# Second layer's local attention: token tiles on the array's row groups instead of heads, keys computed once

## The reference, cut to what matters

```python
def local_gqa_attn(x, wq, wk, wv, wo):
    q = split_heads(x @ wq, H)             # H = 16, HD = 8
    k = split_heads(x @ wk, KVH)           # KVH = 4
    v = split_heads(x @ wv, KVH)
    q, k = (rope(q, BASE_L), rope(k, BASE_L))
    q, k = (qk_norm(q), qk_norm(k))        # x * rsqrt(mean(x * x) + EPS)
    k, v = (repeat_kv(k), repeat_kv(v))
    i = jnp.arange(x.shape[1])
    diff = i[:, None] - i[None, :]
    mask = (diff >= 0) & (diff < WIN)      # WIN = 32
    return merge_heads(sdpa(q, k, v, mask)) @ wo
...
x = x + global_latent_attn(rmsnorm(x, norm1_w), ...)
x = x + local_gqa_attn(rmsnorm(x, norm2_w), ...)
```

## Time and profile before

| | |
|---|---|
| median of 3 runs | 993.89 us (993.09 to 997.41) |
| the profiled execution, its own time | 992.87 us |
| its span (first to last instruction) | 990.7 us, so 2.2 us lie around it |
| TensorE's granted clock in it | 0.996 of 2.4 GHz |
| PE, DVE, ACT, POOL busy | 938.4, 533.3, 539.8, 149.3 us |
| second layer's local attention | heads about 361 to 389, loop 389 to 436, end to about 448 us |

### The profile page before, as it was taken

One profiled execution on the slowest core, in us unless ns is written; L12 is line 12 of the kernel. 1 busy time (PEld: TensorE's weight loads), 2 busy tenths in 40 slices (PEclk: granted clock), 3 DMA queues, 4 the chain that ended last, 5 costly groups with the idle time before them and its releaser, 6 DMA issues.

```text
span 990.7 us, 23062 instructions
## 1 busy us (share of the span) xinstructions
PE 938.4 (95%) x10112; PEld 424.0 (43%) x10112; DVE 533.3 (54%) x870; ACT 539.8 (54%) x767; POOL 149.3 (15%) x164
## 2 busy tenths in 40 slices
PE   7799999999999989889999999989999999999998
PEld 4467643433333335654443444434333333443443
DVE  4566646533324366775665455556666666424554
ACT  6044546889999846646666612275555454545121
POOL 3101120501001003130110400001232232005000
PEclk9999999999999999999999999999999999999999
DMA  7644050100000000000000076000000000002651
GB/s 209 210 123 137 21 225 0 44 2 2 2 2 2 2 1 1 4 3 1 0 1 0 18 169 129 29 1 1 2 2 2 2 2 2 0 1 64 153 118 53
DMA packets 16764, 43.18 MB, mean 44 GB/s; under 512 B 4844, under 2 KB 5292, under 8 KB 15244
## 3 DMA queue, kind: packets, MB, share of 16 engines
q1 hardware_dynamic: 15692, 39.51, 15.0%
q10 hardware_dynamic: 972, 2.20, 0.7%
HBM read 36.91 MB, written 4.55 MB: 42 GB/s over the span
## 4 chain that ended last, share of the span: by engine, by line
PE 79%; ACT 9%; DVE 6%; issue 2%; DMA 2%; SPq 1%; ACTq 0%; POOL 0%; DVEq 0%; POOLq 0%
PE ps L1639 78%; ACT nrr L816 1%; ACT nrr L818 1%; DMA stf<-aux 1%; ACT nsq L809 1%; DVE work L1363 1%; DVE mxq L1258 1%; ACT work L986 1%; ACT work L897 1%; ACT nrr L826 1%; ACT nrr L823 0%; DMA stf<-scr_k 0%; DVE aux L1413 0%; DMA x<-in_x 0%; PE ps L2087 0%
## 5 line engine op out<-in xcount | busy, mean ns | idle before, releaser
L1639 PE MATMUL ps<-rq,stf 32*64 32x512 f32 (+4 forms) x4096 | 197.6, 438 | 6.4 <-DVE stf L1316 2.6
L1639 PE MATMUL ps<-work,vbuf 64*32 64x128 f32 (+6 forms) x2992 | 186.7, 400 | 2.0 <-ACT work L897 1.2
L1639 PE MATMUL ps<-hz,wsb 128*128 128x512 f32 (+1 forms) x352 | 158.4, 599 | 7.0 <-ACT work L1058 4.4
L957 ACT ACTIVATE work<-ps 128x1024 f32<-128x1024 f32 x144 | 139.4, 1023 | 13.2 <-PE ps L1639 8.6
L1639 PEld LDWEIGHTS ps<-rq,stf 32*64 32x64 f32 x4096 | 88.8, 131 | 112.0 <-issue 79.3
L1019 ACT ACTIVATE work<-ps 128x1024 f32<-128x1024 f32 x72 | 73.7, 1025 | 75.6 <-PE ps L1639 75.6
L1639 PEld LDWEIGHTS ps<-work,vbuf 64*32 64x32 f32 (+1 forms) x2992 | 60.0, 107 | 111.1 <-issue 59.1
L1639 PEld LDWEIGHTS ps<-hz,wsb 128*128 128x128 f32 (+1 forms) x352 | 61.6, 186 | 83.4 <-issue 67.9
L1639 PE MATMUL ps<-bsb 128*64 128x512 bf16 (+1 forms) x378 | 82.1, 386 | 11.7 <-DVE mxq L1258 3.8
L1065 ACT ACTIVATE work<-ps 128x512 f32<-128x512 f32 x48 | 28.7, 597 | 117.1 <-PE ps L1639 117.1
L1341 DVE TENSOR_TENSOR work<-work,csb 128x1024 f32<-128x1024 f32 (+1 forms) x40 | 40.7, 1018 | 96.0 <-ACT work L957 95.6
(11 more groups left out here) (200 smaller groups left out, 1167.4 us busy)
## 6 DMA issues: line engine op xcount, KB each, us to landing
stf<-scr_w SPq DMA_DIRECT2D x32, 256.0 KB, 4.7
stf<-scr_w SPq DMA_DIRECT2D x64, 128.0 KB, 3.4
stf<-scr_q SPq DMA_DIRECT2D x12, 192.0 KB
wsb<-in_w SPq DMA_DIRECT2D x1, 2192.0 KB, 12.8
rq<-in_rq SPq DMA_DIRECT2D x2, 1024.0 KB, 10.1
stf<-scr_k SPq DMA_DIRECT2D x9, 204.0 KB
rq<-scr_k SPq DMA_DIRECT2D x6, 204.0 KB
hz<-scr_k SPq DMA_DIRECT2D x6, 204.0 KB
```

The source lines that it names most:

```text
L957: nc.scalar.activation(probs_of(n)[:, 2 * k:2 * k + 2].rearrange("p h s -> p (h s)"), two(slot(2 * n + k)), ACT.Exp, scale=SCALE).then_inc ...
L1639: return nc.tensor.matmul(o, l, r, start=start, stop=stop, skip_group_check=True)
```

## The change

Queries and keys of the local attention are laid out anew: row group j of the 128 partitions holds token tile 4c + j of each chunk c instead of head hd. So the keys, which four heads share, are computed once: two units of KW = 160 columns a tile (32 of the tile before and its own 128), `k_l`, and four query units, one for each head, `q_l`. A score product streams the queries of all four heads. A step's scores are 12 products in place of 32: 64 keys over 4 x 96 queries, 64 keys over 4 x 64, and the 32 keys of the tile before over 4 x 32. All are issued behind both exponentials of the step before. The sums over values change their last part from 64 to 32 rows. The group keys are four masks of 640 columns in place of nine. The rotary table of the second attention is laid out by tile. Nothing else of the program changes. In the diff, UNITS_L is 6 and unit_width is 320 for m < 2 and 512 after; the first `local_heads` shown is DVE's, the second PE's (ACT and POOL have one each of their own).

```diff
-        LOCAL_COUNTS = dict(GLOBAL_COUNTS, sc=32, ex=32, mk=16, pv=16, oe=4, oc=4, o=6)
+        LOCAL_COUNTS = dict(GLOBAL_COUNTS, mm=6, t=6, rot=6, sq=6, var=6, ln=6, r=6, kn=2, kz=4,
+                            sc=32, ex=32, mk=16, pv=16, oe=4, oc=4, o=6)
...
-            rope_load(1)
+            sp.dma_start(rope_l, rope_k.rearrange("k p c s -> p k c s")).then_inc(s_rope, 16)
...
+            def local_heads():
...
+                for m in range(UNITS_L):
+                    rt_, w, o = rope_t[:, m % 4], unit_width(m), pair(AL, m)
...
+                    for i in range(2):
...
+                        ins = nc.vector.tensor_tensor(to, src, turn, ALU.mult)
+                    ins.then_inc(q["t"], 1)
...
+                    if m >= 4:
+                        local_group_keys(m - 4)
...
-                    if n % 2 == 0 and n // 2 + 1 < len(PASSES):
-                        group_keys(AL, *PASSES[n // 2 + 1])
+                    if n < 2:
+                        local_group_keys(2 + n)
...
+            def local_heads():
...
+                def keys(m):
+                    for i in range(2):
+                        for j in range(4):
+                            for k in range(CB):
+                                at = (CB * m + k) * CH + j * P - WIN_L
+                                skip = max(0, -at)
+                                ins = mm(bank(pair(AL, m) + i)[32 * j:32 * j + 32, k * KW + skip:(k + 1) * KW],
+                                         wk[i][:, 0:32], z[:, at + skip:at + KW])
+                    ins.then_inc(q["mm"], 1)
+
+                def queries(m):
+                    hd = m - 2
+                    for i in range(2):
+                        for j in range(4):
+                            ins = mm(bank(pair(AL, m) + i)[32 * j:32 * j + 32].rearrange("p (c s) -> p c s", c=NC),
+                                     wq[i][:, 32 * hd:32 * hd + 32], by_row_group[:, j])
+                    ins.then_inc(q["mm"], 1)
+
+                for m in range(UNITS_L + 1):
+                    if m < UNITS_L:
+                        pe.wait_ge(n_z, normed(n, 2 * m + 1 if m < 2 else NC - 1))
+                        if m >= 3:
+                            pe.wait_ge(q["ln"], was["ln"] + m - 2)
+                        (keys if m < 2 else queries)(m)
+                    if 2 <= m < 2 + NC:
...
+                        values_by_token(v, bank(6 + v % 2), w_("l_wv")).then_inc(q["v"], 1)
+                    if m == UNITS_L:
+                        stay_awake(pair(AL, m - 2) + 1, 5)
+                    if m:
+                        pe.wait_ge(q["sq"], was["sq"] + m)
+                        mm(bank(pair(AL, m - 1))[:, 0:unit_width(m - 1)], c_("head"),
+                           rope_t[:, (m - 1) % 4, 1, 0:unit_width(m - 1)]).then_inc(q["var"], 1)
...
                 def scores(n):
...
+                    if n == 0:
+                        pe.wait_ge(q["q"], was["q"] + G)
...
+                    def block(j, lo, m, q0, w):
+                        rows = slice(32 * j, 32 * j + 32)
+                        o = bank(j)[lo:lo + m, 0:G * W_L].rearrange("p (h s) -> p h s", h=G)
+                        at = HB if m == WIN_L else 0
+                        first = 0 if m == WIN_L else WIN_L + lo
+                        return mm(o[:, :, at:at + w], kz_l[rows, g, c, first:first + m],
+                                  q_l[rows, :, c * P + q0:c * P + q0 + w])
+
+                    if n == 1 or n == 2:
+                        stay_awake(4, 6)
+                    if n:
+                        pe.wait_ge(q["ex"], was["ex"] + 2 * n)
+                    for j in range(4):
+                        block(j, 0, HB, 0, W_L)
+                        block(j, HB, HB, HB, HB)
+                    for j in range(4):
+                        if (n % 2, j) != (0, 0):
+                            ins = block(j, P - WIN_L, WIN_L, 0, WIN_L)
+                        if j % 2:
+                            ins.then_inc(q["sc"], 1)
...
                 def values(n):
...
+                    for j in range(4):
+                        block(j, 0, HB, 4 * st + j, 0, 0, W_L, opens)
+                        ins = block(j, HB, HB, 4 * st + j, HB, 0, HB, opens)
+                    for j in range(4):
+                        if st + j:
+                            ins = block(j, P - WIN_L, WIN_L, 4 * st + j - 1, 0, HB, WIN_L, False)
```

More of the change, by code:

```diff
@@ L49 @@
 W_A, W_L = P + WIN_A, HB + WIN_L
+KW = P + WIN_L
+UNITS_L = 2 + G
 NEG = -1e30
@@ L933, in normed_heads @@
                         ins.then_inc(q["vf"], 1)
-                    if a == AG and 3 <= m < 3 + NC:
+                    if 3 <= m < 3 + NC:
                         hidden_factor(2, m - 3)
+            def local_heads():
+                was = WAS[AL]
+                for m in range(UNITS_L + 1):
+                    if m < UNITS_L:
+                        rt_, w = rope_t[:, m % 4], unit_width(m)
+                        act.wait_ge(q["rot"], was["rot"] + m + 1)
+                        nc.scalar.activation(rt_[:, 1, 0:w], rt_[:, 0, 0:w], ACT.Square).then_inc(q["sq"], 1)
+                    if m:
+                        rt_, w = rope_t[:, (m - 1) % 4], unit_width(m - 1)
+                        act.wait_ge(q["var"], was["var"] + m)
+                        if m > 4:
+                            act.wait_ge(q["kn"], was["kn"] + m - 4)
+                        nc.scalar.activation(rt_[:, 2, 0:w], bank(pair(AL, m - 1))[:, 0:w], ACT.Ln, bias=eps[:, 1:2])\
+                            .then_inc(q["ln"], 1)
+                        act.wait_ge(q["ln"], was["ln"] + m)
+                        nc.scalar.activation(rt_[:, 2, 0:w], rt_[:, 2, 0:w], ACT.Exp, scale=-0.5).then_inc(q["r"], 1)
+                    if 2 <= m < 2 + NC:
+                        c = m - 2
+                        act.wait_ge(q["v"], was["v"] + c + 1)
+                        act.wait_ge(s_vz, 6)
+                        for g in range(NG):
+                            ins = nc.scalar.activation(
+                                vq[:, 4 * c:4 * c + 4, g // 2, g % 2, columns_of(g, False)],
+                                bank(6 + c % 2)[:, 0:4 * KVH * D].rearrange("p (t g d) -> p t g d", t=4, g=NG)
+                                [:, :, g], ACT.Copy)
+                        ins.then_inc(q["vf"], 1)
             def rotated_consumed(a, n):
@@ L1079, in _ @@
             norm(4)
-            normed_heads(AL)
+            local_heads()
             local_soft()
@@ L1812, in normed_heads @@
                             pe.wait_ge(n_z, normed(n, c))
-                        if a == AG and m < 3:
+                        if m < 3:
                             if m == 0:
@@ L1827, in normed_heads @@
                         if v < 2:
-                            pe.wait_ge(n_z, first(n - 1, 2 + v) if a == AG else 4 * n + 3 + v)
+                            pe.wait_ge(n_z, first(n - 1, 2 + v))
                         else:
@@ L1958, in values @@
                     if n == 0:
-                        pe.wait_ge(q["ln"], was["ln"] + 2 * NC)
                         pe.wait_ge(q["vf"], was["vf"] + NC)
@@ L1964, in values, with block @@
                     opens = g % 2 == 0
[L1965 to L1979 removed]
+                    def block(j, lo, m, t, q0, at, w, start):
+                        rows = slice(lo, lo + m)
+                        cells = heads[rows, j, 0:G * W_L].rearrange("p (h s) -> p h s", h=G)
+                        own = qd[rows, T:T + WIN_L] if t < 0 else vq[rows, KT * b + t, g // 2, g % 2]
+                        return mm(by_tile((6 if lo else 4) + st, j)[:, :, q0:q0 + w], own, cells[:, :, at:at + w],
+                                  start, False)
+                    for j in range(4):
+                        block(j, 0, HB, 4 * st + j, 0, 0, W_L, opens)
[3 more added lines that the diff above has]
+                            ins = block(j, P - WIN_L, WIN_L, 4 * st + j - 1, 0, HB, WIN_L, False)
+                        elif opens:
+                            ins = block(j, P - WIN_L, WIN_L, -1, 0, 0, WIN_L, False)
                     ins.then_inc(q["pv"], 1)
@@ L2288, in rope_tables, with turns @@
 def rope_tables():
-    q = np.zeros((2, 2, P, S), np.float32)
-    for n, base in enumerate((1000000.0, 10000.0)):
+    q = np.zeros((2, P, S), np.float32)
+    k = np.zeros((2, P, CB, KW), np.float32)
+    def turns(base, positions):
         inv = np.float32(1.0) / np.float32(base) ** (np.arange(0, D, 2, dtype=np.float32) / np.float32(D))
-        f = np.arange(S, dtype=np.float32)[:, None] * inv.astype(np.float32)[None, :]
-        cos, sin = np.cos(f).astype(np.float32), np.sin(f).astype(np.float32)
-        for row in range(P):
-            d = row % D
-            q[n, 0, row] = cos[:, d // 2]
-            q[n, 1, row] = (-1.0 if d % 2 == 0 else 1.0) * sin[:, d // 2]
-    return q, q[:, :, 0:1, 0:1].copy()
+        f = positions.astype(np.float32)[:, None] * inv.astype(np.float32)[None, :]
```

(13 more changed lines are left out.)

109 lines of the change are left out of this document (56 added, 53 removed).

## The result

The changed kernel takes 1007.27 us in the median (999.94 to 1011.13), the kernel before 993.49 in the runs beside it: a ratio of 1.0114, 95% interval 1.0085 to 1.0143. It is slower by about 11 us. The profiled execution took 1008.33 us.

The account below looks back on a forecast made before the run. PE bounds the heads (19.59 of 20 us); in the loop nobody is full. Heads -3.5, loop +3.0, one slow clock stretch +1.5: +1.0 on 992.87, the runs' median 1.0 above: 995.0 us, range 987 to 1000.5.

Parts of the forecast that it names:

- Heads: Second layer's heads, 8 units become 6: last projection ends at 378.4, first scores at 385.5, 3.5 us earlier.
- The rounds: Query units in the heads: projection 1.73, values 0.86, mean 0.86 and two shape changes at 0.09, 3.63 us each.
- The change of shape: Scores and sums on PE: each change of tile shape costs 0.09 us, behind the widest stream of the old shape.
- rival 1: Loop's scores: changing between 32*64 and 32*32 is free, a step takes 2.48 us, total 986.3; chance 10%.
- Two passes in flight: Loop's scores: eight products' records stream together on PE, so a step's scores are ready 1.25 us after they begin.
- Rival 3: Loop's scores: PE runs products in program order, scores ready after 2.9 us instead of 1.25, total 1021; chance 2%.
- The chain: Attention loop: scores 1.25, two exponentials 1.51 and 0.04 make 2.80 us a step; loop 49.6 us against 46.6.
- doubled sums: Loop steps where two sums over values follow one another (n = 7, 11, 15): PE decides, 3.32 us.
- ACT's wait for PE: Sign in the attention loop: ACT's wait for PE's scores rises from 13.9 to about 20 us.
- The clock: TensorE's clock in this stage: one slow stretch at 1.2 GHz again, costing 1.5 us, as before the change.
- rival 2: The clock falls again and again, each stretch costing 1.5 us, deciding from four on; with five, 1001; chance 20%.
- the sign that I named: Sign for the slower case of repeated clock falls: the loop's window shows a clock under 0.9.

Follow-up runs that it names:

- a1: Changed kernel plus idle bf16 products on PE, 12 ahead of the first scores and three a step from n = 3 on; 999.6 us.
- c3: Version without 32*32 products (992.2 us) plus one more 128x192 exponential a step on ACT, of scores nobody reads; 6.7 us slower than that version.
- b1: Kernel before, with both pairs' scores of a step waiting for both exponentials of the step before; costs that kernel 0.45%.
- d1: Changed kernel, 32*32 products kept, with scores in two pairs of token tiles, each behind its own exponential; 27 us slower than the changed kernel.
- a2: Changed kernel without 32*32 products: 32-key scores issued as 64 keys, last sums over 64 rows; 992.2 us.
- c1: Changed kernel with 32-key scores widened to 64 keys, the sums keeping their 32-row last part; 1000.95 us.
- c2: Changed kernel with last sums over 64 rows, the scores keeping their 32*32 products; 998.7 us.
- f1: Fastest version (no 32*32 products, scores in pairs, 987.6 us) plus one 128*128 bf16 product ahead of each pair's scores; slower than it, clock 0.991.
- f2: Fastest version (no 32*32 products, scores in pairs, 987.6 us) with one token tile's two score products reissued in each pair; slower than it, clock 0.995.
- f3: Fastest version (no 32*32 products, scores in pairs, 987.6 us) with the sums' last products back at 32*32, 32 rows deep; 992.1 us.
- g1: Changed kernel with twelve idle bf16 products ahead of its first scores and nothing else; total within the expected 1003 to 1006 us.

## Why the prediction was wrong

The forecast was 995.0 us and no measurable change; the kernel takes 1007.3 and is slower by 1.1%. Step by step:

- *Heads.* The rounds are 3.80 us (377.12 to 380.92) instead of 3.63. The last projection, forecast to end at 378.4, ends near 382.7 (380.92 and its 1.73), of which 3.6 us is this execution's late arrival. The first scores come 22.6 us after the norm's last product instead of 25.4: 2.7 us won, where I had 3.5. Right in kind, 0.8 short.
- *The change of shape.* 0.09 us was right. The gap between the last start of the old shape and the first of the new, less the old one's streaming, is 91 ns from 32*64 to 32*32 and 92 ns from 64*32 to 32*32 in the trace after. The first 32*32 record starts 0.83 us behind the step's first, forecast 0.78, and 0.5 by rival 1, which falls.
- *Two passes in flight.* Right: scores are ready 1.28 us after they begin, forecast 1.25. Rival 3 falls.
- *The chain.* 2.83 to 2.92 us a step, forecast 2.80; doubled sums 3.46, forecast 3.32; the loop at full clock 51.0, forecast 49.6. Right in kind, 1.4 short. ACT's wait for PE, forecast at 20 us, is 31.1, the surplus being the clock's.
- *The clock.* **"I reckon with one stretch again, at 1.5"** is the step that failed. There are 30.7 us at half clock in the profile, as much as nine stretches of before's 3.4, and they cost 11.1 us (the estimate above) where I put 1.5. That the clock is what costs is shown by a1: with the clock held up, the same program and more products are 7.7 us faster. This is rival 2, slower, for which I had 20%: "each stretch costs 1.5; it decides from four on" was right as a rule (11.1 over nine is 1.2 each), and a clock of 0.76 in the loop's window is the sign that I named. I counted one stretch because the kernel before had one with similar idle time. It was no measure: the trace of before has no 32*32 product, and what those do to the clock no row of it shows.

The terms that were off are 0.8 in the heads, 1.4 in the chain and 9.6 in the clock: 11.8 of the 12.3 us between forecast and median. They come from one profile, whose execution took 1008.3; the changed kernel's four runs lie between 999.9 and 1011.1, so that they match so closely is partly luck.

The reason that I gave for rival 2, idleness, was half of it. Waiting longer lowers the clock (c3, b1), but PE fully busy did not save it (d1), and idling twice as long did not hurt it (a2). The 32*32 products count beside it. Sorted by them, the profiles have at half clock: with 32*32 products both in the scores and in the sums 6.8 to 68.3 us except where idle full-array products stand between them (a1: none), in one of them 3.4 to 27.3, in none 0 to 17.1. These ranges overlap, and each figure is one profile. That 32*32 products cost the clock is shown by the runs of c1 and c2 against a2 and after; by what property of theirs is open. Changes of shape alone (f1) and a partly used array for part of a pair (f2) did not do it at the sizes tried. How the two combine was not tried.

One rival that I overlooked takes in idleness and narrow products together: how much of the array streams in the mean. It can be estimated from the program and the traces. A 384-wide float32 record streams for 0.32 us (384 x 2 / 2.4 GHz) and two records make a product; a 32*64 or 64*32 product takes an eighth of the array and a 32*32 product a sixteenth. A step of the changed kernel then has 1.17 us of the whole array, and one with 64-key scores and sums 1.28. Over their steps that is 0.34 of the array in d1, 0.41 after, 0.45 in c3 and 0.49 in a2, and the clocks of their runs are in the same order: 0.963, 0.985, 0.989, 0.994. It would explain why d1 lost the clock without idling and why a2 kept it. But c1 (0.47, clock 0.983) and f3 (0.55, 0.989), with 32*32 products in the sums alone, have lower clocks than their share would put them at. No run varies this share alone, so it stays open.

## What to carry to other kernels

A small product of its own tile shape can cost more than its records. Here it was its 0.09 us twice, the overlap of what stands on either side of it, and above all the clock of everything around it. Try padding it to its neighbours' shape, even if it then computes zeros: in this kernel that was worth 15 us of the 1007. And a busy share near 100% is no proof of a full clock; when PE's work is cut into smaller tiles, read the granted clock of that window before anything else, and give a fall of it a term of its own size, not the size it had before.

Where two halves of a step use different row groups and different exponentials, let each wait for its own. Together with the padding this turned the change from 1.1% slower into 0.7% faster.

## What the runs showed of the hardware

- TensorE's granted clock stood at 1.2 GHz from 415 to 476.4 us while PE had work in flight all the time (d1: busy 43.00 of 43.00 and 17.85 of 17.85 us). Ahead of it PE had been busy 15.00 of 15.00 us at 2.4 GHz.
- The long stretches at 1.2 GHz in this stage are all in kernels with 32*32 products (61.5 us in d1, 37.5 in g1, 27.3 in c1, 20.5 after). All other stretches, in kernels with and without such products, are 3.4 or 6.8 us.
- A change of tile shape holds back everything behind it, also on row groups that the old shape did not use: two pairs of scores on different row groups take 1.12 us together (f3), 2.27 with a shape change behind each (d1).
- The price of a change was the same where rows stay the same and columns halve (32*64 to 32*32, 91 ns), and where rows halve (64*32 to 32*32, 92 ns), both in the trace after.
